# Cross-attention and a routed attention layer on one core: the order of operations around the routed attention and in the opening

## Chip, cores and metric

One core of a Trainium2 chip. The metric is the device time of one execution in microseconds (us); 64 batches are computed in it. Matrix products are done in float32 with operands split into two float32r parts ("hi" and "lo"), three products each.

## The reference

For each of 64 batches, x is 256 x 256 and the context 77 x 192. Layer 1 is cross-attention with 8 heads of 64; layer 2 is a causal attention whose queries, keys and values are mixed from 16 experts by routing weights.

```python
x = x + xattn(layernorm(x), ctx, Wq, Wk, Wv, Wo, bo)      # softmax(q k^T / 8) v, then Wo
h = layernorm(x)
logits = normalize(h) @ normalize(sim) - sigmoid(gates)   # 16 experts
rw = softmax of relu(logits) over the active experts (or the top 2 where none is)
q, k, v = [sum over e of rw[e] * (h @ proj[e]) for proj in (q_proj, k_proj, v_proj)]
attn = causal_softmax(q k^T / 8) v                        # one head of 64
x = x + sum over e of (attn * rw[e]) @ o_proj[e]
```

## The kernel before

The kernel is written engine by engine: each of the five engines has its own program, and every engine's order of work is written out by hand in a function `step(i)`, run for i = -2 to 65. Engines meet only in semaphores. Every engine works strictly through its list, so an operation that waits holds all that stands behind it on that engine. In step i the operations belong to batches i+2 (`nxt`), i+1 (`ahead`), i (`now`), i-1 (`before`) and i-2 (`earlier`), and where a batch does not exist they are left out.

**The cross-attention (names with a_)** is folded: for each group of three batches "jobs" turn the context into G (wq times keys) and U (values times Wo), which go through memory (`g_dram`, `u_dram`) and come back batch by batch as `gq` and `uo`. There are 25 jobs a group: ct, k 0 to 3, v 0 to 3, g 0 to 7, u 0 to 7. They are spread over the slots E0, E1, E2, E3, M1, M2, M3, L1, L2 of three consecutive steps by the table `JOBS`; a slot is run by `turn(...)`. Jobs g 3 to 7 fall in steps with i % 3 = 0, u 0 to 5 in those with i % 3 = 1, and u 6, u 7, k 0 to 2 and g 0 to 2 in those with i % 3 = 2. The A banks of PSUM (three) go round the slots in the order of `A_ORDER`, and `freed` waits for whoever held the bank before: S1 to S3, PT0 to PT2, XT, Y and the job slots share them. The bank of E3 is that of PT0 before it and of M2 behind it; PT1's passes to M1.

For one batch: ln1_a (bn_stats of `xt`, L1066) and ln1_b (L1081) normalise x, a_xT transposes it (XT), a_s 0 to 3 are the scores (S0 to S3), whose maximum DVE takes (L1163) and whose exponentials ScalarE takes (a_exp, L893); a_psum (L1170) gives the reciprocals of the sums, GpSimd multiplies (a_p, L1506), a_pT transposes (PT0 to PT2, L598, drained at L1175 and L1179), and a_y multiplies by `uo` (Y) and adds x.

**The routed attention.** ln2_a, ln2_b and b_norm normalise; b_xT transposes into banks of the B ring (L632); b_qkv 0 to 15 are the projections of two experts and one of the two token tiles each (L467 to L469), drained by DVE with the routing weights as factors (L1232 for 0 and 1, L1235 for the rest, two operations each). The B ring has three banks for 18 fills a batch, so b_qkv 3 waits until b_qkv 0 is drained, and b_xT 1 until b_qkv 14 of the batch before is. b_top (largest logits), b_index and GpSimd's b_route_1, b_route_2, b_w (L1476), then DVE's b_wsum (L1216, L1218) and GpSimd's b_rw (L1482) give the weights. c_qk transposes q and k (L658; four copies on ScalarE, two on DVE, L1246), c_s are the scores (L666), c_exp and c_p the softmax, c_pT its transpose (L674, drained at L1241), c_pv the product with v, c_mix 0 to 3 the products with the weights, and c_y the output projection, two steps later.

**The queues.** SyncE (SP) issues the loads and stores in order and waits in order: `load_x(n)` (L348), `load_ctx` (L358, L359), `store_g` (L364), `store_u` (L373), `load_g(n)` (L383, waits for all stores of G of the group), `load_u(n)` (L390 to L394, waits for all stores of U of the group), `store` (L399). ScalarE's queue issues the two small transfers that spread the routing weights over the partitions (`c_rT`, `c_rw`, L945 and L952).

**The opening.** Before step -2 the 25 jobs of group 0 are run in the order of `OPENING`, while the 16 weight pieces (`PIECES`: 0 to 5 the cross-attention's, 6 to 13 the experts' projections, 14 and 15 o_proj) are loaded into three staging areas and split into hi and lo (`split_weights`, L824 on ScalarE and L1051 on DVE) at the places that `SPLIT_AFTER` gives. A piece can be loaded only when the piece three before it is split.

Of the kernel before, what the change touches and what calls it, by code (L numbers as in the profile page):

```python
# [34 lines left out]
def xattn_moe_kernel(nc, x, ctx_in, Wq, Wk, Wv, Wo, bo, sim_matrix, gates, q_proj, k_proj, v_proj, o_proj, out, rw_dram):  # L35
# [63 lines left out]
    def on(n):  # L99
        return 0 <= n < B  # L100
# [14 lines left out]
    with es:  # L115
# [216 lines left out]
        def loads_before(piece):  # L332
# [4 lines left out]
                       ("u", 0): (9,), ("u", 2): (10,), ("u", 7): range(11, len(PIECES))}  # L337
# [5 lines left out]
        def _(sp):  # L343
# [33 lines left out]
            def load_g(n):  # L377
                gm, b = n // GB, n % GB
                for k in range(2):
                    sp.wait_ge(draft_out[k], stored(gm) + 16 * (H // 2))  # L380
                if n:
                    sp.wait_ge(s_fill, at(2 * NT, n - 1, 3))
                sp.dma_start(gq[:, :, :, :, :].rearrange("p a b c d -> p (a b c d)").bitcast(F32), g_dram[gm, b, :, :]).then_inc(g_in, 16)  # L383
# [35 lines left out]
            def step(i):  # L419
# [13 lines left out]
                if on(i + 2):  # L433
                    load_g(i + 2)
                turn("E1")
                if i % 3 == 2 and on(i + 1):
                    load_u(i + 1)
# [16 lines left out]
            for hc, pieces in enumerate(((12,), (13,), (), (14, 15))):  # L454
                store_u(0, 2 * hc)
                store_u(0, 2 * hc + 1)
                load_weights(pieces)
            for i in range(-2, B + 2):
                step(i)
# [4 lines left out]
        def _(pe):  # L464
# [270 lines left out]
            def step(i):  # L735
                nxt, ahead, now, before, earlier = [i + d for d in (2, 1, 0, -1, -2)]

                def do(n, fn, *k):
                    if on(n):
                        fn(n, *k)  # L740
# [55 lines left out]
                do(now, b_qkv, 1)  # L796
                do(before, c_s)
                do(now, b_qkv, 2)
                fill("Y", ahead, a_y, 0)
                do(before, c_pT)  # L800
                do(ahead, a_y, 1)
                do(before, c_pv)
                do(now, b_qkv, 3)
# [10 lines left out]
        def _(act):  # L814
# [164 lines left out]
            def step(i):  # L979
                nxt, ahead, now, before, earlier = [i + d for d in (2, 1, 0, -1, -2)]  # L980

                def do(n, fn, *k):
                    if on(n):
                        fn(n, *k)
# [16 lines left out]
                do(before, c_rT)  # L1001
                do(ahead, a_exp, 0)
                do(ahead, a_exp, 1)
                do(ahead, a_exp, 2)
                do(ahead, a_exp, 3)
                turn("E1")
# [4 lines left out]
                do(ahead, a_pT, 2)  # L1011
                turn("E3")
# [3 lines left out]
                do(nxt, a_xT)  # L1016
                turn("M2")
                do(before, c_qk)
                turn("M3")
                do(before, c_exp)  # L1020
# [15 lines left out]
        def _(dve):  # L1036
# [247 lines left out]
            def step(i):  # L1284
# [22 lines left out]
                do(before, b_qkv, 7)  # L1307
                do(now, ln2_a)
                do(ahead, a_s, 0)
                do(before, b_qkv, 8)  # L1310
                do(ahead, a_s, 1)
                do(now, ln2_b)
                do(before, b_qkv, 9)
                do(ahead, a_s, 2)
                do(now, b_norm, 0)
                do(before, b_qkv, 10)
                do(now, b_norm, 1)
                do(ahead, a_psum, 0)
                do(ahead, a_s, 3)
                do(now, b_norm, 2)  # L1320
                do(ahead, a_psum, 1)
                do(before, b_qkv, 11)
                turn("E1")
                do(earlier, c_y)
                turn("E2")
                do(nxt, ln1_a)
                do(before, b_qkv, 12)
# [3 lines left out]
                do(ahead, a_pT, 2)  # L1331
                do(nxt, ln1_b)
                do(before, b_qkv, 14)
                turn("E3")
                do(before, b_qkv, 15)
# [3 lines left out]
                do(nxt, a_xT)  # L1339
                turn("M2")  # L1340
                do(before, c_qk)
                do(now, b_top)
                do(before, c_s)
                do(now, b_index)
                do(before, c_p)
                turn("M3")
                do(before, c_pT)
# [3 lines left out]
                do(ahead, a_y)  # L1351
                do(before, c_mix, 0)
                do(now, b_qkv, 2)
                do(before, c_mix, 1)
                do(now, b_qkv, 3)
                do(before, c_mix, 2)
                do(now, b_qkv, 4)
# [212 lines left out]
```

## Time and profile before

| | |
|---|---|
| median of 3 runs | 2813.47 us (2812.5 to 2815.11) |
| the profiled execution | 2814.86 us, its span 2813.1 us |
| busy share of the span | PE 90%, DVE 78%, ACT 49%, POOL 39% |
| matmuls, transposes among them | 17308 |
| memory traffic | 157 GB/s over the span |
| chain that ended last | PE 59%, DVE 19%, ACT 12%, issue 7%, DMA 2%, POOL 1% |

PE is TensorE, DVE VectorE, ACT ScalarE, POOL GpSimd, SP SyncE. In the rows, `L1246` is a line of the kernel; "[0.93 <-DVE mixs_hi L1246]" says that the engine stood for 0.93 us and that the named instruction let it go ("issue" is a wait whose releaser the profile doesn't show, such as a load that landed). PEclk is the granted clock of TensorE as a share of 2.4 GHz; 0.50 is 1.2 GHz.

### The profile page before, as it was taken

How to read it: one execution, taken by the hardware profiler on the slowest of the kernel's cores; microseconds unless marked ns; L12 is line 12 of the kernel's file. 1: busy time of each engine (PE TensorE's matmuls, PEld its weight loads, DVE VectorE, ACT ScalarE, POOL GpSimd, SP SyncE). 2: the span in 40 equal slices, each digit the busy share in tenths (PEclk: the TensorE clock that was granted, in tenths of full speed). 3: DMA queues.
4: the chain of work that ended last, by engine and by line, in shares of the span. 5: the costliest groups of instructions: out<-in, count | busy, mean ns of one | idle time of the engine just before them, and what ended most of it. 6: DMA issues, size and time to landing. Idle time of an engine off the chain costs nothing.

```text
span 2813.1 us, 53794 instructions
## 1 busy us (share of the span) xinstructions
PE 2528.2 (90%) x17308; PEld 2427.3 (86%) x17308; DVE 2201.7 (78%) x6491; ACT 1378.8 (49%) x4598; POOL 1103.9 (39%) x1611
## 2 busy tenths in 40 slices
PE   4599999999999899999999999999989999999987
PEld 3589889889889889889889989988989988988986
DVE  5488888888888777878878878888778888888874
ACT  4454454555455454455455545545445455545531
POOL 0134344434434434434434434433434433443442
PEclk6699999999999999999999999999999999999998
DMA  7555555464555455455555555465555446455531
GB/s 188 186 158 169 172 165 160 139 189 142 172 170 161 149 165 164 137 184 154 168 163 169 155 157 177 133 186 155 169 159 163 156 146 189 139 173 167 161 91 41
DMA packets 299936, 445.75 MB, mean 158 GB/s; under 512 B 36857, under 2 KB 210873, under 8 KB 291465
## 3 DMA queue, kind: packets, MB, share of 16 engines
q1 hardware_dynamic: 230024, 374.15, 41.5%
q10 hardware_dynamic: 69632, 68.17, 10.9%
q8 instruction: 140, 2.29, 0.3%
q14 instruction: 140, 1.14, 0.1%
HBM read 257.91 MB, written 184.35 MB: 157 GB/s over the span
## 4 chain that ended last, share of the span: by engine, by line
PE 59%; DVE 19%; ACT 12%; issue 7%; DMA 2%; POOL 1%; SPq 0%; DVEq 0%; ACTq 0%; POOLq 0%
PE bank_b L467 9%; PE bank_b L469 8%; PE bank_b L468 8%; DVE acc L1235 5%; PE bank_a L467 4%; PE bank_c L467 4%; PE bank_c L469 4%; PE bank_c L468 4%; PE bank_a L468 4%; PE bank_a L469 4%; DVE both L1136 2%; DVE pT_lo L1179 2%; DVE probs L1081 2%; ACT both L852 1%; ACT both L851 1%
## 5 line engine op out<-in xcount | busy, mean ns | idle before, releaser
L467 PE MATMUL bank_b<-wqkv_hi,x2T_lo 128*128 128x384 f32 (+1 forms) x2048 | 724.7, 354 | 18.4 <-DVE acc L1232 18.1
L1235 DVE SCALAR_TENSOR_TENSOR acc<-bank_b,rw,acc 128x192 f32<-128x192 f32 x1792 | 659.7, 410 | 61.5 <-PE bank_b L469 54.9
L469 PE MATMUL bank_b<-wqkv_hi,x2T_hi 128*128 128x384 f32 (+1 forms) x2048 | 692.2, 338 | 0.0
L468 PE MATMUL bank_b<-wqkv_lo,x2T_hi 128*128 128x384 f32 (+1 forms) x2048 | 690.8, 337 | 0.0
L1511 POOL TENSOR_TENSOR mixs_lo<-mix,mixs_hi 128x512 fp32r<-128x512 f32 x256 | 404.1, 1609 | 227.0 <-ACT mixs_hi L961 227.0
L893 ACT ACTIVATE probs<-bank_a,s_max 128x77 f32<-128x77 f32 x1024 | 317.3, 330 | 281.8 <-DVE s_max L1163 279.2
L467 PEld LDWEIGHTS bank_b<-wqkv_hi,x2T_lo 128*128 128x128 f32 x2048 | 386.6, 189 | 29.5 <-DVE acc L1232 26.8
L468 PEld LDWEIGHTS bank_b<-wqkv_lo,x2T_hi 128*128 128x128 f32 x2048 | 387.9, 189 | 0.0
L469 PEld LDWEIGHTS bank_b<-wqkv_hi,x2T_hi 128*128 128x128 f32 x2048 | 384.6, 188 | 0.0
L1506 POOL TENSOR_TENSOR probs<-probs,p_sum 128x616 f32<-128x616 f32 x128 | 155.8, 1217 | 356.9 <-DVE p_sum L1170 356.9
L467 PE MATMUL bank_c<-wo_hi,mixs_lo 128*128 128x256 f32 x1024 | 288.6, 282 | 3.7 <-POOL mixs_lo L1511 3.7
L1436 POOL TENSOR_TENSOR pow_out<-pow_in,expo 128x2 f32<-128x2 f32 (+1 forms) x128 | 111.4, 871 | 452.2 <-DVE pow_in L1073 315.9
L469 PE MATMUL bank_c<-wo_hi,mixs_hi 128*128 128x256 f32 x1024 | 288.1, 281 | 0.0
L468 PE MATMUL bank_c<-wo_lo,mixs_hi 128*128 128x256 f32 x1024 | 287.7, 281 | 0.0
L961 ACT ACTIVATE mixs_hi<-mix 128x512 fp32r<-128x512 f32 x256 | 161.7, 632 | 231.4 <-DVE mix L1276 231.4
L1136 DVE TENSOR_TENSOR both<-bank_a,only 64x231 fp32r<-64x231 f32 x352 | 139.2, 395 | 141.3 <-ACT both L852 139.0
L1276 DVE TENSOR_TENSOR mix<-rw_all,late_tiles 128x512 f32<-128x512 f32 x256 | 231.8, 906 | 2.2 <-ACT late_tiles L957 2.1
L893 ACT ACTIVATION_READ_ACCUMULATOR probs<-bank_a,s_max 128x1 f32 x1024 | 215.4, 210 | 0.0
L467 PE MATMUL bank_a<-uo,pT_lo 128*128 128x256 f32 (+1 forms) x640 | 189.2, 296 | 18.1 <-issue 17.9
L467 PEld LDWEIGHTS bank_c<-wo_hi,mixs_lo 128*128 128x128 f32 x1024 | 193.4, 189 | 4.1 <-issue 3.8
L468 PEld LDWEIGHTS bank_c<-wo_lo,mixs_hi 128*128 128x128 f32 x1024 | 194.2, 190 | 0.0
L469 PEld LDWEIGHTS bank_c<-wo_hi,mixs_hi 128*128 128x128 f32 x1024 | 193.5, 189 | 0.0
(204 smaller groups left out, 6161.7 us busy)
## 6 DMA issues: line engine op xcount, KB each, us to landing
g_dram<-draft SPq DMA_DIRECT2D x176, 462.0 KB
gq<-g_dram SPq DMA_DIRECT2D x64, 1232.0 KB, 5.5
uo<-u_dram SPq DMA_DIRECT2D x64, 1024.0 KB
rw_all<-rw_dram ACTq DMA_DIRECT2D x128, 512.0 KB, 7.4
u_dram<-draft SPq DMA_DIRECT2D x176, 308.0 KB
xt<-in_x_dram SPq DMA_DIRECT2D x64, 256.0 KB, 3.9
out_dram<-mix SPq DMA_DIRECT2D x64, 256.0 KB, 6.2
u_dram<-draft SPq DMA_DIRECT2D x88, 156.0 KB
```

The costliest lines, as they stand in the source:

```text
L467: nc.tensor.matmul(dst, lhs[1], rhs[0], start=start, stop=False)
L468: nc.tensor.matmul(dst, lhs[0], rhs[1], start=False, stop=False)
L469: return nc.tensor.matmul(dst, lhs[0], rhs[0], start=False, stop=stop)
L893: last = nc.scalar.activation(probs[:, t, h * NC:(h + 1) * NC], bank_a(f"S{j}")[:, k * NC:(k + 1) * NC], ACT.Exp, bias=s_max[:, j, k:k + 1 ...
L961: nc.scalar.activation(mixs[0][:, 2 * j:2 * j + 2, :], mix[:, 2 * j:2 * j + 2, :], copy).then_inc(mix_hi, 1)
L1081: V.tensor_scalar(dst[:, t, :], src[:, t, :], mv[k][:, t, 0:1], pow_out[k][:, 0, t:t + 1], ALU.subtract, ALU.mult).then_inc(ln_done[k], 1)
L1136: last = V.tensor_tensor(both[rows, k, e, cols], src[rows, cols], only.bitcast(F32)[rows, k, e, cols], ALU.subtract)
L1235: V.scalar_tensor_tensor(acc[:, t, k, :], src, rw[:, t, e:e + 1], acc[:, t, k, :], ALU.mult, ALU.add).then_inc(b_evac, 1)
L1276: V.tensor_tensor(mix[:, 2 * j:2 * j + 2, :], rw_all[:, 2 * j:2 * j + 2, :], aT2[:, :].unsqueeze(1).to_broadcast([P, 2, T]), ALU.mult).the ...
L1436: G.tensor_tensor(dst, src, expo[:, 0:m], ALU.pow).then_inc(ln_pow[k], 1)
L1506: G.tensor_tensor(part, part, p_sum[:, half, 1, :, :].unsqueeze(3).to_broadcast([P, NT, HB, NC]), ALU.mult).then_inc(p_ready, 1)
L1511: G.tensor_tensor(mixs[1][:, 2 * j:2 * j + 2, :], mix[:, 2 * j:2 * j + 2, :], mixs[0].bitcast(F32)[:, 2 * j:2 * j + 2, :], ALU.subtract).t ...
```

## The change

No operation is added or removed and none changes its engine; orders change, in three places.

- On PE: b_qkv 2 goes ahead of c_s, c_pT behind both halves of Y, b_qkv 3 ahead of c_pv. On ScalarE: c_qk goes ahead of slot M2.
- On DVE: a_s 0 ahead of ln2_a; ln2_b two places later; ln1_a of the batch after next from behind slot E2 to the place between a_s 3 and the second a_psum; b_qkv 12 ahead of slot E2; ln1_b and b_qkv 15 ahead of slot E3 (ln1_b now behind b_qkv 14); c_qk ahead of M2; b_index ahead of c_s; c_pT from ahead of b_wsum to behind a_y; b_qkv 2, 3 and 4 each one place earlier among the c_mix.
- In the opening: pieces 11 to 15 are split inside step -1 instead of before step -2, on ScalarE and DVE; pieces 14 and 15 are loaded during step -1; load_g(0) is issued behind the stores of G and load_u(0) behind the stores of U.

```diff
--- before.py
+++ after.py
@@ -334,7 +334,7 @@
 
 
         SPLIT_AFTER = {("k", 1): (W_V,), ("k", 2): (W_O - 1, W_O), ("k", 3): (6,), ("v", 0): (7,), ("v", 1): (8,),
-                       ("u", 0): (9,), ("u", 2): (10,), ("u", 7): range(11, len(PIECES))}
+                       ("u", 0): (9,), ("u", 2): (10,)}
 
         block = es.enter_context(nc.Block())
 
@@ -430,10 +430,14 @@
                 turn("E0")
                 if on(i + 2) and i + 2 > 0:
                     load_x(i + 2)
-                if on(i + 2):
+                if i == -1:
+                    load_weights((14,))
+                if on(i + 2) and i + 2 > 0:
                     load_g(i + 2)
+                if i == -1:
+                    load_weights((15,))
                 turn("E1")
-                if i % 3 == 2 and on(i + 1):
+                if i % 3 == 2 and on(i + 1) and i + 1 > 0:
                     load_u(i + 1)
                 if on(i - 2):
                     store(i - 2)
@@ -451,10 +455,12 @@
                 store_g(0, 2 * hc)
                 store_g(0, 2 * hc + 1)
                 load_weights(pieces)
-            for hc, pieces in enumerate(((12,), (13,), (), (14, 15))):
+            load_g(0)
+            for hc, pieces in enumerate(((12,), (13,), (), ())):
                 store_u(0, 2 * hc)
                 store_u(0, 2 * hc + 1)
                 load_weights(pieces)
+            load_u(0)
             for i in range(-2, B + 2):
                 step(i)
             sp.wait_ge(y_out, 16 * B)
@@ -794,13 +800,13 @@
                 do(now, b_qkv, 0)
                 turn("M3")
                 do(now, b_qkv, 1)
+                do(now, b_qkv, 2)
                 do(before, c_s)
-                do(now, b_qkv, 2)
                 fill("Y", ahead, a_y, 0)
+                do(ahead, a_y, 1)
                 do(before, c_pT)
-                do(ahead, a_y, 1)
+                do(now, b_qkv, 3)
                 do(before, c_pv)
-                do(now, b_qkv, 3)
                 do(now, b_qkv, 4)
                 turn("L1")
                 do(now, b_qkv, 5)
@@ -999,24 +1005,34 @@
 
                 turn("E0")
                 do(before, c_rT)
+                if i == -1:
+                    split_weights(11)
                 do(ahead, a_exp, 0)
                 do(ahead, a_exp, 1)
                 do(ahead, a_exp, 2)
                 do(ahead, a_exp, 3)
+                if i == -1:
+                    split_weights(12)
                 turn("E1")
                 turn("E2")
                 do(ahead, a_pT, 0)
                 do(ahead, a_pT, 1)
                 do(before, c_rw)
                 do(ahead, a_pT, 2)
+                if i == -1:
+                    split_weights(13)
                 turn("E3")
                 do(now, b_xT, 0)
                 do(now, b_xT, 1)
                 turn("M1")
                 do(nxt, a_xT)
+                if i == -1:
+                    split_weights(14)
+                do(before, c_qk)
                 turn("M2")
-                do(before, c_qk)
                 turn("M3")
+                if i == -1:
+                    split_weights(15)
                 do(before, c_exp)
                 do(now, b_exp)
                 do(before, c_pT)
@@ -1305,56 +1321,66 @@
                 do(before, b_qkv, 6)
                 turn("E0")
                 do(before, b_qkv, 7)
+                if i == -1:
+                    split_weights(11)
+                do(ahead, a_s, 0)
                 do(now, ln2_a)
-                do(ahead, a_s, 0)
                 do(before, b_qkv, 8)
                 do(ahead, a_s, 1)
-                do(now, ln2_b)
                 do(before, b_qkv, 9)
                 do(ahead, a_s, 2)
-                do(now, b_norm, 0)
+                do(now, ln2_b)
                 do(before, b_qkv, 10)
-                do(now, b_norm, 1)
                 do(ahead, a_psum, 0)
                 do(ahead, a_s, 3)
+                do(now, b_norm, 0)
+                do(nxt, ln1_a)
+                do(now, b_norm, 1)
+                do(ahead, a_psum, 1)
                 do(now, b_norm, 2)
-                do(ahead, a_psum, 1)
                 do(before, b_qkv, 11)
+                if i == -1:
+                    split_weights(12)
                 turn("E1")
                 do(earlier, c_y)
+                do(before, b_qkv, 12)
                 turn("E2")
-                do(nxt, ln1_a)
-                do(before, b_qkv, 12)
                 do(ahead, a_pT, 0)
                 do(ahead, a_pT, 1)
                 do(before, b_qkv, 13)
                 do(ahead, a_pT, 2)
+                if i == -1:
+                    split_weights(13)
+                do(before, b_qkv, 14)
                 do(nxt, ln1_b)
-                do(before, b_qkv, 14)
+                do(before, b_qkv, 15)
                 turn("E3")
-                do(before, b_qkv, 15)
                 do(now, b_xT, 0)
                 do(now, b_xT, 1)
                 turn("M1")
                 do(nxt, a_xT)
+                if i == -1:
+                    split_weights(14)
+                do(before, c_qk)
                 turn("M2")
-                do(before, c_qk)
                 do(now, b_top)
+                do(now, b_index)
+                if i == -1:
+                    split_weights(15)
                 do(before, c_s)
-                do(now, b_index)
                 do(before, c_p)
                 turn("M3")
-                do(before, c_pT)
                 do(now, b_wsum)
                 do(now, b_qkv, 0)
                 do(now, b_qkv, 1)
                 do(ahead, a_y)
+                do(before, c_pT)
+                do(now, b_qkv, 2)
+                do(now, b_qkv, 3)
                 do(before, c_mix, 0)
-                do(now, b_qkv, 2)
                 do(before, c_mix, 1)
-                do(now, b_qkv, 3)
+                do(now, b_qkv, 4)
                 do(before, c_mix, 2)
-                do(now, b_qkv, 4)
                 do(before, c_mix, 3)
                 turn("L1")
                 do(now, b_qkv, 5)
```

## Rows read from the trace of the kernel before

**Rows 1.** The cores: span and mean granted clock of PE.

```profile
core 0: 2813.1 us, clock 0.978
```

**Rows 2.** PE's waits from 300 to 2650 us: total us, times, longest us.

```profile
PE bank_c L666 <- DVE mixs_hi L1246: 52.6, 56, 1.5
...
PE bank_b L632 <- DVE acc L1235: 47.8, 56, 0.9
...
PE bank_a L467 <- issue: 13.5, 16, 2.5
```

**Rows 3.** PE in order of time, kind 1: start, us, line, operation, [idle before <- releaser].

```profile
1042.31 0.38 PE L577 MATMUL bank_a<-wo,both 128*116 128x256 f32 x1 [0.83 <-DVE pT_lo L1179]
...
1047.21 0.41 PE L658 MATMUL bank_c<-ident,mix 128*128 128x128 f32 x2
```

**Rows 4.** DVE in order of time, the same step.

```profile
1039.60 0.75 DVE L1066 BATCH_NORM_STATS2 stats<-xt 128x6 f32<-128x256 f32 x2
...
1040.92 0.74 DVE L1235 SCALAR_TENSOR_TENSOR acc<-bank_b,rw,acc 128x192 f32<-128x192 f32 x2
```

**Rows 5.** PE, DVE and POOL in order of time, from c_s to b_qkv 3 of that step.

```profile
1051.20 0.30 PE L666 MATMUL bank_c<-mixs_hi 128*128 128x128 f32 x1 [0.93 <-DVE mixs_hi L1246]
...
1057.75 0.44 PE L467 MATMUL bank_b<-wqkv_hi,x2T_lo 128*128 128x384 f32 x1 [0.27 <-DVE acc L1232]
...
1055.68 0.56 DVE L1241 TENSOR_TENSOR mixs_lo<-bank_c,mixs_lo 128x384 fp32r<-128x384 f32 x1 [0.79 <-ACT mixs_lo L917]
...
1056.95 1.39 DVE L1232 TENSOR_SCALAR acc<-bank_b,rw 128x192 f32<-128x192 f32 x4 [0.42 <-POOL rw L1482]
...
1055.36 0.25 POOL L1476 TENSOR_TENSOR w<-w,act_on 128x32 f32<-128x32 f32 x1
```

**Rows 6.** SP, DVE, POOL and PE in a kind-2 step; then that x load's time to landing.

```profile
1073.94 0.40 SPq L348 DMA_DIRECT2D xt<-in_x_dram  x1
...
1078.58 0.66 SPq L373 DMA_DIRECT2D u_dram<-draft  x2
...
1088.08 0.38 SPq L392 DMA_DIRECT2D uo<-u_dram  x1
...
1074.29 0.48 DVE L1163 TENSOR_REDUCE s_max<-bank_a 128x4 f32<-128x308 f32 x1
...
1076.45 1.22 POOL L1506 TENSOR_TENSOR probs<-probs,p_sum 128x616 f32<-128x616 f32 x1 [0.80 <-DVE p_sum L1170]
...
1080.06 0.81 PE L598 MATMUL bank_a<-ident,probs 128*128 128x128 f32 x6
...
1095.13 0.35 PE L467 MATMUL bank_a<-uo,pT_lo 128*128 128x256 f32 x1 [0.98 <-issue]
...
1100.15 0.44 PE L467 MATMUL bank_b<-wqkv_hi,x2T_lo 128*128 128x384 f32 x1 [0.31 <-DVE acc L1232]
...
DMA to landing us min/median/max: 5.4/5.4/5.4
```

**Rows 7.** SP in a late kind-2 step; then the DMA queues from 1083 to 1085 us.

```profile
2459.50 0.66 SPq L373 DMA_DIRECT2D u_dram<-draft  x2
...
2465.91 0.38 SPq L392 DMA_DIRECT2D uo<-u_dram  x1
...
q10 hardware_dynamic: 440, 0.44, 96.5%
...
q1 hardware_dynamic: 51, 0.10, 13.1%
```

**Rows 8.** PE at Y of an earlier kind-2 step; then 969 to 974: busy us, PEclk, DMA share, GB/s.

```profile
968.51 0.36 PE L467 MATMUL bank_a<-uo,pT_lo 128*128 128x256 f32 x1 [2.52 <-issue]
...
969.00:974.00 5.00, 5.00 (x31) 5.00 (x31) 1.37 (x5) 0.49 (x1) 0.24 (x1) 0.66 0.04 12
```

**Rows 9.** PE and SP in the opening.

```profile
92.69 0.62 PE L467 MATMUL bank_a<-gq,xT_lo 128*128 128x308 f32 x1 [12.02 <-DVE cT_lo L1130]
...
89.62 0.39 SPq L348 DMA_DIRECT2D xt<-in_x_dram  x1
```

## The prediction

> **What bounds the kernel now.** I read the size of the run first: one core, 2813.1 us of span [rows 1]. The profiled execution took 2814.86 us around that span, 1.4 above the median of 2813.47; I work out a difference and take it from the median. TensorE (PE) is busy for nine tenths, so the second view is who PE waits for. Over 56 of the 64 steps [rows 2] three waits matter: c_s for VectorE's (DVE's) part of c_qk, 0.94 us a step; the transpose b_xT for the bank that b_qkv 14 leaves, 0.85 a step; and, about once in three steps, the attention product Y for the load of `uo`, 0.84. Steps come in three kinds by i % 3, which have different jobs of the context group in their slots; I call them kind 0, 1 and 2. A kind-1 step was followed instruction by instruction [rows 3 to 5], then a kind-2 step [rows 6].
>
> **Part 1, the stretch before b_xT (all kinds).** DVE drains PT0 late, because ln1_a of the batch after next (1.3 us, from 1039.60 to 1040.92), and b_qkv 12 after it, stand ahead of it [rows 4]. So PE stands 0.83 us in front of slot E3 and then 0.85 for the bank of b_qkv 14 [rows 2, 3]. The change puts ln1_a in front of the second reciprocal, where DVE otherwise waits for ScalarE's exponentials, and drains b_qkv 12 before slot E2 while ScalarE still works for it: that takes 1.9 us of DVE work out of the queue ahead of PT0, and both PE waits (1.7 us) go. What is late next: E3's result is now drained behind ln1_b and b_qkv 15, three times 0.6 to 0.75 us (the pair of acc operations in [rows 4] takes 0.74, and I take that for each), 2.0 us after b_qkv 14's, while PE needs E3's bank again at M2, two short jobs (about 1.0 us) after b_xT 1. A new wait of up to 0.9, less the 0.4 that c_qk gains because its sums on GpSimd (POOL) are ready first: net gain in kind 1, 1.2 us. In kind 0 the wait at E3 is nearly absent, but b_xT's wait and 0.3 in front of c_qk go: also 1.2.
>
> **Part 2, from c_qk to b_qkv 4.** PE does b_qkv 2 before c_s, which covers c_s's wait of 0.93, and ScalarE and DVE do c_qk before M2's job. But b_qkv 3 needs the bank of b_qkv 0, which DVE drains only with the routing weights: POOL's last product (1055.36 to 1055.61), DVE's sum, POOL's rw, then acc at 1056.95, and PE at 1057.75 [rows 5]. Before, that chain is held only by c_pT on DVE, from 1055.68 to 1056.16: moving c_pT behind a_y gives the chain 0.5 us and no more. And c_pv (three products, about 0.5 us) now follows b_qkv 3 and can no longer fill that wait. So PE loses its wait at c_s and gets one of about 1.6 in front of b_qkv 3: net 0 in kind 1, and 0.4 in kind 0, where b_index now comes ahead of c_s and gives POOL's chain its input sooner. c_pT on PE behind the whole of Y costs nothing while c_p takes less than Y's 3.5 us.
>
> **Part 3, kind 2.** ln1_a needs x of batch i+2, which SP loads in the same step, behind four context loads and two stores: issued at 1073.94, landed 5.4 us later, at 1079.3. The score maximum that stands ahead of ln1_a in the new order begins at 1074.29, so DVE arrives at 1074.7 and stands for 4.6 us [rows 6]. Queued behind it on DVE are the second reciprocal, b_qkv 11, slot E1 (which in this kind is u 7, the last of the group), c_y, b_qkv 12. Two things follow. POOL's product (1076.45, 1.22 us long) comes after 1080.6 + 0.3, so PT0 on PE moves from 1080.06 to 1082.4. And u 7 is drained and stored 3.8 us later than 1078.58. Only once all stores of the group have landed (1088.08) does SP load `uo`, which lets Y start at 1095.13 after 0.98 us of waiting [rows 6]. The store takes 9.5 us in this step, 6.4 in one of the last steps, which has no context loads [rows 7]. Bounds for Y: 3.8 + 6.4 - 9.5 = 0.7 later, and 3.8 later. I take 2.2, since the end of the store is tied to the `rw_all` loads on ScalarE's queue, which move with PT0 (2.3): while they run, they hold 96.5% of the engines and SP's queue 13.1% [rows 7].
>
> The Trainium skill ("DMA: Bandwidth & Descriptors", section on queues, rings and completion order) says that each DMA engine takes turns between the queues it has work for. By that rule the store would get a full share beside `rw_all` and land near the lower bound; the row at 13.1% is too small for even turns, but does not say whether the store had more to send.
>
> After Y, b_qkv 3 followed 5.0 us later in the old order (1100.15), held by the acc chain. With Y late that chain is long done: Y and c_pT take 3.9, so b_qkv 4 comes 0.6 sooner after Y than before. Loss in kind 2: 2.2 - 0.6 = 1.6 us, with bounds 0.1 and 3.2. Parts 1 and 2 gain nothing here, since Y's wait swallows what lies ahead of it. On top comes the clock. Where Y had waited 2.52 us, granted clock was 0.66 over the next 5 us, that is half rate (1.2 GHz) for a part of them, which costs 5 x 0.34 = 1.7 us [rows 8]. New waits here are 2.3 at PT0 and about 3.6 at Y. If the clock already falls after PT0, its cost vanishes in Y's wait; so bounds are 0 and 1.7, and I take 0.9.
>
> **Part 4, opening and end.** Five weight pieces are split inside step -1 rather than before step -2, and o_proj is loaded during it. DVE was behind them for the 12.02 us that S0 of batch 0 waited [rows 9]: that is the upper bound of the gain. But load_u(0) now stands on SP ahead of the context and x loads and waits for u 7's store, so x of batch 1 is issued about when it was before (89.62), and the new ln1_a waits for it ahead of the reciprocal. I take 4 us; the lower bound is a loss of 3, the five splits not fully hidden. At the end, the last two steps load no x and gain 2 together. Part 4: 6. The new issue order on SP costs nothing else; the exceptions at i == -1 move existing DMAs and add none.
>
> **Sum.** 20 kind-0 steps x 1.6 = 32 and 21 kind-1 steps x 1.2 = 25 gained; 20 kind-2 steps x (1.6 + 0.9) = 50 lost; 6 gained: net 13, so 2813.5 - 13 = 2801 us, 0.4% faster. Two large terms nearly cancel, so the sign hangs on kind 2.
>
> **Rivals.**
> A, the store of u 7 gets through (it no longer queues behind the 1.2 MB of `gq`; the page's rule speaks for it): kind 2 loses 0.1 and the wait stays short enough for the clock. 57 + 6 - 2 = 61 gained, 2752; with part of the late landing, 2765. Against it: `rw_all` begins sooner after that store than before. Chance 0.24.
> B, the other side: DVE's stop for x in kind 2 passes in full to Y, and PE's wait of 4 to 5 us drops the clock each time. 20 x (3.2 + 1.7) = 98 lost against 63: 35 slower, 2848. It decides from the point where kind 2 costs over 3.2 us a step (63 / 20). For it: clock did fall after each wait that I can show of over 2.4 us. Against: that store takes 6.4 us where nothing crowds it. Chance 0.27.
> C, parts 1 and 2 return as waits in full (M2 for E3's bank, b_qkv 3 for routing), so that kinds 0 and 1 gain only half: 28 + 6 - 34 = 0, with kind 2 somewhat milder at 1.7: no change, 2813. Chance 0.13.
> The forecast itself has 0.36, with a range of its own of 2788 to 2818.
>
> **How the numbers follow.** About 0.2% (5.6 us) is what a measurement of this kernel tells from no change. Faster by more than that: A whole (0.24), two thirds of the forecast (0.25), some of C (0.04): 0.53. Slower: B nearly whole (0.25), a sixth of the forecast (0.04) and C (0.03): 0.32. Same: 0.15. The range reaches from A to B, 2755 to 2845; about a tenth lies outside at each end.
>
> **What would show it.** Right: no PE wait for acc in front of b_xT and none for c_qk in front of c_s; instead one of some 1.6 us in front of b_qkv 3 in kinds 0 and 1, and up to 0.9 at M2. In kind 2, DVE idle for about 4.6 us in front of bn_stats of `xt`, released by the x load, PT0 released late by POOL, and Y's wait at 3 to 4 us with half-rate clock behind it in part of the steps. Period of three steps: 0.3 to 0.6 us shorter. Wrong: if x lands before DVE asks (then all kinds gain and the time is under 2755), if Y's start in kind 2 hardly moves (A), or if the clock also falls after the 1.6 us in front of b_qkv 3, where I count nothing: that would put the time above the range.

## The result and the profile after

The changed kernel takes 2932.47 us (median of 4 runs, 2928.24 to 2934.9) where the kernel before took 2812.98 beside it: ratio 1.0427, 95% interval 1.0406 to 1.0448. It is 4.3% slower; the forecast was 0.4% faster, and the time lies above the range.

The cores, then the busy times of the profiled execution (2933.07 us, its span 2931.2):

```profile
core 0: 2931.2 us, clock 0.945
...
PE 2606.9 (89%) x17308; PEld 2513.0 (86%) x17308; DVE 2321.8 (79%) x6491; ACT 1387.0 (47%) x4598; POOL 1085.2 (37%) x1611
```

Beside the 2813.1 us and the clock of 0.978 of before [rows 1], the span grew by 118.1 us. PE has the same 17308 instructions, and yet it is busy for 2606.9 us instead of 2528.2. **78.7 us of the 118.1 are the same products taking longer; only 39.4 are more standing still.** The first is the sign of the clock. PE's waits show both:

```profile
PE bank_a L473 <- issue: 72.1, 19, 4.6
PE bank_b L473 <- DVE acc L1248: 64.6, 37, 1.8
PE bank_a L604 <- POOL probs L1532: 19.3, 13, 2.5
PE bank_c L473 <- DVE mixs_lo L1257: 18.7, 52, 0.4
PE bank_a L571 <- DVE both L1152: 11.2, 19, 0.7
PE bank_a L546 <- DVE draft L1174: 10.1, 19, 0.5
PE bank_b L638 <- DVE acc L1251: 5.3, 17, 0.4
...
PE bank_c L680 <- DVE mix L1285: 1.2, 4, 0.5
```

(From 300 to 2760 us: total, times, longest. Lines are 6 higher than before on PE: L473 is the projection, Y and c_pv products, L604 PT0, L638 b_xT, L672 c_s, L680 c_pT; the bank_c line at L473 is c_pv.) Against [rows 2], the two largest waits of before are gone: c_s does not wait at all, and b_xT waits 5.3 us instead of 47.8. Their place is taken by Y, 3.8 us in each of 19 steps of kind 2, and by b_qkv 3, 1.75 us in each of 37 steps of kinds 0 and 1. Close behind it c_pv waits for DVE's drain of c_pT, 0.36 us in 52 steps. In order of time, a step of kind 0:

```profile
1051.53 0.52 PE L680 MATMUL bank_c<-ident,mix 128*128 128x128 f32 x3 [0.52 <-DVE mix L1285]
1053.54 0.69 PE L473 MATMUL bank_b<-wqkv_hi,x2T_lo 128*128 128x384 f32 x1 [1.49 <-DVE acc L1248]
1054.03 0.52 PE L474 MATMUL bank_b<-wqkv_lo,x2T_hi 128*128 128x384 f32 x1
1054.35 0.52 PE L475 MATMUL bank_b<-wqkv_hi,x2T_hi 128*128 128x384 f32 x1
```

The products of b_qkv 3 start 0.32 us apart and take 0.52, where they start 0.18 apart and take 0.34 a few microseconds later. The windows view says why (us, busy time of each engine, PEclk, DMA share, GB/s; first around b_qkv 3, then around Y of the kind-2 step before it, which starts at 1006.27 after 3.98 us):

```profile
1048.00:1053.00 5.00, 3.54 (x30) 3.12 (x28) 3.07 (x18) 1.60 (x6) 3.04 (x12) 1.00 0.48 112
1053.00:1058.00 5.00, 4.46 (x19) 4.46 (x20) 4.11 (x11) 0.38 (x1) 0.00 (x0) 0.66 0.66 237
1058.00:1063.00 5.00, 5.00 (x37) 4.96 (x36) 5.00 (x8) 2.83 (x5) 4.08 (x3) 1.00 0.01 3
...
1000.00:1005.00 5.00, 2.30 (x15) 2.09 (x13) 3.95 (x19) 1.86 (x7) 2.13 (x9) 1.00 1.02 305
1005.00:1010.00 5.00, 3.73 (x17) 3.76 (x18) 1.82 (x7) 0.00 (x0) 0.99 (x4) 0.56 0.50 164
1010.00:1015.00 5.00, 4.78 (x29) 4.49 (x28) 1.94 (x5) 0.49 (x1) 0.00 (x0) 0.76 0.10 26
```

A PEclk of 0.66 over 5 us is half rate (1.2 GHz) for a part of them, and takes 5 x 0.34 = 1.7 us from PE, the same loss as in [rows 8]; behind Y it is 2.2 + 1.2 = 3.4. I cut the span from 200 to 2690 us into windows of half a microsecond and summed what each lacked in PEclk: before, 2 such stretches and 3.4 us lost; after, **46 stretches and 97.2 us lost**. The loss is 1.7 or 3.4 each time. (It is above the 78.7 us of busy time; part of it falls where PE stands anyway.) Set beside PE's waits, 23 of the 46 lie at b_qkv 3, 19 at Y and 4 at PT0, where PE stands for 2.4 to 2.5 us in those steps of kind 2.

The third view is the mean time from one c_s to the next, by the kinds of the two steps (21 of each):

| kernel | 2 to 0 (holds kind 2's Y) | 0 to 1 | 1 to 2 |
|---|---|---|---|
| before | 42.01 | 41.61 | 41.03 |
| after | 43.86 | 42.35 | 44.12 |

The sum over three steps grew by 5.7 us, 21 times 5.7 = 119: the whole loss is in the steps, and none of it in the opening or at the end.

### The profile page after: what moved, and what is told of

Read it like the earlier page. It is cut to its first block, busy times and chain, and to the rows that moved or that the text cites. A ratio compares the mean times of both kernels' runs of the same rounds, so it can differ in the third digit from the quotient of the medians.

```text
span 2931.2 us, 53794 instructions
## 1 busy us (share of the span) xinstructions
PE 2606.9 (89%) x17308; PEld 2513.0 (86%) x17308; DVE 2321.8 (79%) x6491; ACT 1387.0 (47%) x4598; POOL 1085.2 (37%) x1611
## 4 chain that ended last, share of the span: by engine, by line
PE 58%; DVE 12%; issue 11%; ACT 7%; POOL 6%; ACTq 3%; DMA 2%; SPq 0%; DVEq 0%; POOLq 0%
PE bank_b L473 8%; PE bank_b L475 8%; PE bank_b L474 8%; PE bank_c L473 5%; PE bank_c L475 4%; PE bank_c L474 4%; PE bank_a L473 4%; PE bank_a L474 4%; PE bank_a L475 4%; ACTq L958 3%; DVE acc L1251 2%; POOL probs L1532 1%; PE bank_a L604 1%; DVE probs L1097 1%; ACT pT_hi L909 1%
## 5 line engine op out<-in xcount | busy, mean ns | idle before, releaser
L473 PE MATMUL bank_b<-wqkv_hi,x2T_lo 128*128 128x384 f32 (+1 forms) x2048 | 742.7, 363 | 74.9 <-DVE acc L1248 74.6
L475 PE MATMUL bank_b<-wqkv_hi,x2T_hi 128*128 128x384 f32 (+1 forms) x2048 | 705.6, 345 | 0.0
L474 PE MATMUL bank_b<-wqkv_lo,x2T_hi 128*128 128x384 f32 (+1 forms) x2048 | 702.9, 343 | 0.0
L1537 POOL TENSOR_TENSOR mixs_lo<-mix,mixs_hi 128x512 fp32r<-128x512 f32 x256 | 380.7, 1518 | 457.6 <-ACT mixs_hi L967 457.6
L473 PEld LDWEIGHTS bank_b<-wqkv_hi,x2T_lo 128*128 128x128 f32 x2048 | 397.0, 194 | 86.7 <-DVE acc L1248 84.8
L1292 DVE TENSOR_TENSOR mix<-rw_all,late_tiles 128x512 f32<-128x512 f32 x256 | 275.0, 1115 | 30.1 <-ACT late_tiles L963 30.1
L473 PE MATMUL bank_c<-wo_hi,mixs_lo 128*128 128x256 f32 x1024 | 288.7, 282 | 3.7 <-POOL mixs_lo L1537 3.7
L473 PE MATMUL bank_a<-uo,pT_lo 128*128 128x256 f32 (+1 forms) x640 | 200.9, 314 | 81.5 <-issue 80.9
L1517 POOL TENSOR_TENSOR mix<-acc 128x192 f32<-128x192 f32 x128 | 82.1, 641 | 427.2 <-DVE acc L1251 427.1
L473 PEld LDWEIGHTS bank_a<-uo,pT_lo 128*128 128x128 f32 (+1 forms) x640 | 140.8, 220 | 85.4 <-issue 84.6
L474 PE MATMUL bank_a<-uo,pT_hi 128*128 128x256 f32 (+1 forms) x640 | 197.8, 309 | 0.0
L475 PE MATMUL bank_a<-uo,pT_hi 128*128 128x256 f32 (+1 forms) x640 | 197.1, 308 | 0.0
```

Source lines behind the costliest of these rows:

```text
L473: nc.tensor.matmul(dst, lhs[1], rhs[0], start=start, stop=False)
L474: nc.tensor.matmul(dst, lhs[0], rhs[1], start=False, stop=False)
L475: return nc.tensor.matmul(dst, lhs[0], rhs[0], start=False, stop=stop)
L1292: V.tensor_tensor(mix[:, 2 * j:2 * j + 2, :], rw_all[:, 2 * j:2 * j + 2, :], aT2[:, :].unsqueeze(1).to_broadcast([P, 2, T]), ALU.mult).the ...
L1517: G.tensor_tensor(qkv[:, t, :], acc[:, t, 0, :], acc[:, t, 1, :], ALU.add).then_inc(qkv_ready, 1)
L1537: G.tensor_tensor(mixs[1][:, 2 * j:2 * j + 2, :], mix[:, 2 * j:2 * j + 2, :], mixs[0].bitcast(F32)[:, 2 * j:2 * j + 2, :], ALU.subtract).t ...
```

## The experiments

Twelve runs, in the order that the argument needs. Every time stands beside runs of the kernel before on the same chip, which had medians of 2812.6, 2813.8 and 2817.4 us in the three groups of runs; where runs of different groups are set against each other, I take ratios times 2813.5. Lists of PE's waits count from 300 to 2650 us unless another stretch is named.

**open_only: the opening alone (Part 4).** The kernel before with the changes of the opening, on SP, ScalarE and DVE, and with no change in the order of the steps.

```diff
-                if on(i + 2):
+                if on(i + 2) and i + 2 > 0:
                     load_g(i + 2)
...
+            load_g(0)
...
+                if i == -1:
+                    split_weights(11)
```

> Only the opening of the change (pieces 11 to 15 split in step -1, loads of o_proj, gq and uo reordered), all else as before. The clock theory and the x-load theory both put the loss in the steps: 2812, within 4 us of before, since the first c_s of the changed kernel came only 0.3 us sooner (172.70 against 172.98). A theory that the opening costs would want 10 us or more above before.

Measured: 2807.74 us (10 runs), ratio 0.9986 (0.9975 to 0.9997), clock 0.979. The opening gives about 4 us, as predicted, at the edge of what can be told from no change.

**mid_only: the middle alone (Part 2).** The kernel before with the new orders from M1 to L2; PE's part is shown, and ScalarE's and DVE's are those of the change.

```diff
                 do(now, b_qkv, 1)
+                do(now, b_qkv, 2)
                 do(before, c_s)
-                do(now, b_qkv, 2)
                 fill("Y", ahead, a_y, 0)
+                do(ahead, a_y, 1)
                 do(before, c_pT)
-                do(ahead, a_y, 1)
+                do(now, b_qkv, 3)
                 do(before, c_pv)
-                do(now, b_qkv, 3)
```

> Only the orders from M1 to L2 (b_qkv 2 ahead of c_s, c_pT behind Y, b_qkv 3 ahead of c_pv on PE; c_qk ahead of M2 on ScalarE and DVE; DVE's c_pT behind a_y). Clock theory: the waits of PE add up to about what they were, but one of about 1.6 us now stands in front of b_qkv 3, and the clock falls to half behind it in many steps: 30 to 80 us slower, 2845 to 2890, mean granted clock about 0.955. x-load theory (all the loss comes from ln1_a standing for x in the third kind of step): within 10 us of before, clock 0.978.

Measured: 2909.87 us, ratio 1.0342 (1.0322 to 1.0363), clock 0.955. PE's wait at b_qkv 3 from 300 to 2700 us:

```profile
PE bank_b L467 <- DVE acc L1232: 65.3, 41, 1.8
```

PE is busy for 2589.3 us, 61 more than before, and 31 half-rate stretches lose 63.1 us. So the part that I had put at a gain of 8 us costs 97: 61 of it in the clock, and 36 in PE standing more. That is over the 30 to 80 us expected. The 36 lie at c_pv, which waits 15.8 us where it waited for nothing, at Y, 31.8 us for 13.5, and in an exchange of c_s for b_qkv 3 that gained next to nothing (68.0 us for the two together before, 63.1 now, in fewer steps).

**early_only: DVE's early orders alone (Parts 1 and 3).** The kernel before with DVE's new order from E0 to M1, ln1_a early in all kinds.

> Only DVE's orders up to M1 (ln1_a early, b_qkv 12 ahead of E2, E3 behind b_qkv 15). Both theories: kinds 0 and 1 gain about 1.2 us a step (50 us); kind 2 loses about 2 us in front of Y and up to 3.4 by the clock. Clock theory: 2815 to 2860. x-load theory, which has to find 119 us here: 2900 or more.

Measured: 2868.63 us, ratio 1.0191 (1.0174 to 1.0208), clock 0.962; 25 half-rate stretches, 56.3 us lost. From 300 to 2700 us Y waits 58.3 us in 19 steps, and c_s 64.1 in 56. The time is 9 us above the expected 2815 to 2860, and 31 below the 2900 of the theory that all the loss lies here. The two parts alone, 97 + 56, are more than the 119 of the whole, so they are not independent; from here on they are taken one after the other.

**ln_late_k2: the changed kernel with ln1_a late in kind 2.** In that kind ln1_a goes back behind slot E2; all else is as changed.

```diff
-                do(nxt, ln1_a)
+                if i % 3 != 2:
+                    do(nxt, ln1_a)
...
                 turn("E2")
+                if i % 3 == 2:
+                    do(nxt, ln1_a)
                 do(ahead, a_pT, 0)
```

> The changed kernel with DVE's ln1_a early only in kinds 0 and 1, and in kind 2 (i % 3 = 2) where it was before. Clock theory: Y's wait in kind 2 falls back to about 1 us, but b_qkv 3's wait and its clock stay in kinds 0 and 1: 2810 to 2860. x-load theory: all that is lost comes back and the gain of the other steps shows: 2760 or less.

Measured: 2858.1 us, ratio 1.0172 (1.014 to 1.0205), clock 0.956. The one operation that stands for x in kind 2 costs 72 us by the ratios, 3.4 per kind-2 step, where Part 3 had 2.5 (1.6 and 0.9). The wait at b_qkv 3 is untouched (65.9 us in 38, from 300 to 2700 us), and 28 half-rate stretches are left, 20 at b_qkv 3 and 8 at Y.

**early_k01: the early orders in kinds 0 and 1, the middle as before.** The opening, DVE's early orders with ln1_a as in the run above, and the middle of the kernel before on all engines.

> Opening of the change, DVE's orders up to M1 with ln1_a early in kinds 0 and 1 only, and the orders from M1 to L2 as before the change. Clock theory: keeps the 1.2 us a step of part 1 and puts no wait over 1.5 us anywhere: 2750 to 2775, clock 0.975 or more. x-load theory the same. If part 1 by itself calls up dips of the clock (PE's two short waits now closer together in front of c_s): 2790 to 2830.

Measured: 2787.89 us (5 runs, 2775.07 to 2789.98), ratio 0.9886 (0.9868 to 0.9905), clock 0.974: faster than both kernels, though less than expected. What Part 1 gave at b_xT partly came back at c_s:

```profile
PE bank_c L672 <- DVE mixs_hi L1262: 64.3, 56, 3.2
PE bank_a L473 <- issue: 22.3, 19, 2.6
PE bank_b L473 <- DVE acc L1248: 14.7, 52, 0.5
```

b_xT waits only 5.7 us in 19 steps, but c_s waits 64.3 us where it waited 52.6 [rows 2]. These runs form a chain from before to after, each with one part more: opening -4; early orders in kinds 0 and 1 -28; the middle +80; ln1_a early in kind 2 +72. Together +120. (The last two are good to about 10 us by the intervals.) PE's busy time takes 43 of the 80 and 25 of the 72.

**filler: is it the clock?** The changed kernel with eight useless 384-column products on PE behind c_pT in every step, so that PE works while it would stand at b_qkv 3.

```diff
                 do(before, c_pT)
+                do(before, filler, 8)
                 do(now, b_qkv, 3)
```

> The changed kernel with 8 extra products of 384 columns on PE behind c_pT (about 0.17 us each, 1.4 us in all, written into the bank that c_pv overwrites), so that PE works through the wait in front of b_qkv 3. The work is useless and the waits of the other engines stay. Clock theory: the time lost by the clock behind b_qkv 3 goes, some 25 to 30 dips of 1.7 us: 2870 to 2890, although PE does 11 us x 8 more work (88 us busy). Theory that the waits themselves cost the time (the clock being only a mark of them): 2932 or more, up to 3000.

Measured: 2926.55 us, ratio 1.0404 (1.0388 to 1.042), clock 0.966. The expected 2870 to 2890 is missed, and the profile says by what:

```profile
PE bank_a L473 <- issue: 69.6, 18, 4.5
PE bank_a L604 <- POOL probs L1538: 37.3, 17, 2.8
...
PE bank_b L473 <- DVE acc L1254: 11.5, 33, 0.4
```

The wait at b_qkv 3 is nearly gone and half-rate stretches fell from 46 to 22 (44.4 us lost instead of 97.2), but 64 x 1.42 = 91 us of work were added, a third of it in kind 2, where b_qkv 3 doesn't wait, and PT0's wait doubled. Gain and price nearly cancel; as a test of the clock it is inconclusive by its time alone. The next two are cleaner.

**filler_k01: the same products in kinds 0 and 1 only.**

```diff
                 do(before, c_pT)
+                if i % 3 != 2:
+                    do(before, filler, 8)
```

> The changed kernel, with 8 useless products behind c_pT in the steps of kinds 0 and 1 only. The run with them in every step gave 2926.6 us: its waits at b_qkv 3 fell from 64.6 to 11.5 us and half-rate stretches from 46 to 22, but 64 times 1.45 us of products were added, 21 of these where nothing waited, and the 17 waits at the first transpose of the probabilities grew from 19.3 to 37.3 us. Theory: without the products of kind 2 the run gives back 21 x 1.45 = 30 us and perhaps the 18 us of the longer wait: 2878 to 2900 us, under the changed kernel's 2932 by 32 to 54 us although 43 x 1.45 = 62 us of useless work were added and only some 55 us of waiting taken out; the rest is the clock, 35 to 60 us. Rival (the clock is not worth anything by itself): within 10 us of the changed kernel, 2922 to 2942 us.

Measured: 2910.97 us, ratio 1.0335 (1.0317 to 1.0354), clock 0.963. The expected 2878 to 2900 is missed by 11 us, since PT0's wait stayed at 36.6 us instead of falling back: so it doesn't come from kind 2's products. That it comes from kinds 0 and 1 becoming faster is likely, but not shown. In sum: 43 x 1.45 = 62 us of products added, 52 of waiting at b_qkv 3 taken out, 17 more at PT0, and 51 fewer lost to the clock (46.1 in 23 stretches), which gives 24 less than the changed kernel; by the ratios it is 26. None of the 23 stretches left lies at b_qkv 3 (19 at Y, 4 at PT0). PE is busy for 2621.4 us, only 14.5 more than in the changed kernel, although 62 us of products were added: the other products took 48 us less. Adding useless work made the kernel faster.

**fill_y: the clock by itself.** The changed kernel with 20 such products in front of Y in kind 2, written to Y's own bank, which Y overwrites. Y waits for a load, so products that fit into its wait move nothing else.

```diff
+                if i % 3 == 2 and i > 0:
+                    fill("Y", ahead, filler, 20)
                 fill("Y", ahead, a_y, 0)
```

> The changed kernel, with 20 useless 384-column products put in front of Y in the steps of kind 2 (i % 3 == 2, from the third step on), into Y's own bank, which Y overwrites. In the changed kernel the 19 waits at Y between 300 and 2760 us take 72.1 us, 3.8 each, and what Y waits for is the load of uo, which TensorE does not set; 20 such products take about 3.5 us (8 took 1.5 in the run with the filler behind c_pT). So they fit into the wait and move nothing: what changes is only that TensorE works while it would stand. Theory (the stand itself costs the clock): the half-rate stretch behind Y, which costs 1.7 to 3.4 us in each step of kind 2, goes. 21 of them, 36 to 70 us: 2862 to 2897 us against the changed kernel's 2932; the mean granted clock rises from 0.945 to over 0.958. Rival (the clock falls for another reason, such as the load or the work as a whole): 2928 to 2940 us, clock under 0.95.

Measured: 2894.41 us, ratio 1.0279 (1.026 to 1.0299), clock 0.964: 42 us less than the changed kernel by the ratios, in the slower half of what the theory gave, with 21 x 3.66 = 77 us of work added. PE in order of time at one Y, then the windows around it, then the waits:

```profile
993.56 3.66 PE L686 MATMUL bank_a<-wqkv_hi,x2T_hi 128*128 128x384 f32 x20
997.64 0.36 PE L473 MATMUL bank_a<-uo,pT_lo 128*128 128x256 f32 x1 [0.42 <-issue]
...
999.00:1004.00 5.00, 4.77 (x38) 4.48 (x37) 2.85 (x8) 0.55 (x2) 0.00 (x0) 1.00 0.33 71
...
PE bank_b L473 <- DVE acc L1255: 64.2, 37, 1.8
...
PE bank_a L473 <- issue: 9.6, 17, 1.1
```

Nearly all of it is in the stretch that holds Y: from 43.86 us to 42.15 (2 to 0), while 0 to 1 (42.14) and 1 to 2 (44.15) differ by 0.2 us or less from the changed kernel. Y begins no sooner, counted from the load of x (24.6 us in the median of both). Half-rate stretches fell from 46 to 23, and 47.8 us are lost instead of 97.2. All 23 left lie at b_qkv 3. The two fillers split the 46 in two: those at Y and PT0 go when Y's wait is filled, those at b_qkv 3 when that one is.

**pv_first: c_pv ahead of b_qkv 3 again.** The changed kernel with this one order of PE undone, to see whether c_pv covers the wait as it did before.

```diff
-                do(now, b_qkv, 3)
                 do(before, c_pv)
+                do(now, b_qkv, 3)
```

> The changed kernel with c_pv ahead of b_qkv 3 on PE again (c_pT still behind Y, DVE's c_pT still behind a_y). Clock theory: c_pv has to wait for DVE's a_y and c_pT, so the wait moves in front of c_pv and stays at over 1 us; 0.5 us a step less: 2880 to 2915. If the place of c_pv alone is at fault: 2860 or less.

Measured: 3042.23 us, ratio 1.0812 (1.0796 to 1.0829), clock 0.935: 108 us slower than the changed kernel by the ratios, against my expectation of 2880 to 2915.

```profile
PE bank_c L473 <- DVE mixs_lo L1257: 144.0, 52, 3.6
```

c_pv needs DVE's drain of c_pT. The change put that drain behind a_y on DVE and c_pT behind Y on PE, so c_pv waits 2.8 us, and b_qkv 3 stands behind it; 62 half-rate stretches lose 131.4 us. I had moved one engine's order back and left the other two: an order on PE and the order of the drains on DVE are one thing.

**top_first: how long must the wait be?** As ln_late_k2, and DVE drains M2 only behind c_p, so that b_top starts POOL's routing chain sooner.

```diff
                 do(before, c_qk)
-                turn("M2")
                 do(now, b_top)
...
                 do(before, c_p)
+                turn("M2")
                 turn("M3")
```

> The changed kernel with ln1_a late in kind 2 and DVE's drain of slot M2 moved from ahead of b_top to behind c_p, so that the chain b_top, GpSimd's routing, b_wsum, rw, acc starts 0.6 to 1.3 us sooner. Theory that this chain sets b_qkv 3 and its wait sets the clock: the wait in front of b_qkv 3 falls from 1.7 to under 1 us and the dips in kinds 0 and 1 go: 2730 to 2780. If c_pT or the a_y drain ties b_qkv 3 instead: within 20 us of the 2858 of the run with ln1_a late alone.

Measured: 2809.48 us (11 runs), ratio 0.9993 (0.9983 to 1.0003), clock 0.972. It is 50 us faster than ln_late_k2 by the ratios, and 29 above the expected 2730 to 2780:

```profile
PE bank_b L473 <- DVE acc L1248: 49.5, 37, 1.5
PE bank_a L473 <- issue: 39.2, 19, 4.3
```

The wait at b_qkv 3 is 1.34 us each instead of 1.73, which is 15 us in all, and half-rate stretches fell from 28 to 14: from 20 to 7 at b_qkv 3, from 8 to 7 at Y. PE's busy time fell by 39.5 us. The chain of [rows 5] does set b_qkv 3, and with its wait 0.4 us shorter the clock fell there a third as often.

**qk_early and qk_top_early: the best of both.** The first is early_k01 with c_qk drained ahead of M2 on ScalarE and DVE; the second also has DVE's drain of M2 behind c_p.

```diff
+                do(before, c_qk)
                 turn("M2")
-                do(before, c_qk)
                 do(now, b_top)
```

> The run with the early orders in kinds 0 and 1 and the middle as before (2787.9 us), with one thing of the changed kernel's middle added: ScalarE and VectorE drain c_qk ahead of M2's bank. That run's largest wait of TensorE is c_s for the drain of c_qk, 64.3 us in 56 waits between 300 and 2650, 1.15 each. Theory (this wait can go without a price, since c_s stands behind b_qkv 1 and b_qkv 3 behind c_pv as before): c_s's wait falls under 10 us, M2's bank comes back later and costs under 10, b_qkv 3 waits no more than 0.5 us a time: 2730 to 2755 us, clock 0.97 to 0.98, faster than both kernels. Rival (the wait moves on to another place, since VectorE has as much to do): 2775 to 2795 us, with a wait of 0.8 us or more a step at b_qkv 3, Y or the key products.

> As the run before it, and on VectorE b_top, c_s and b_index also ahead of M2's drain, which moved behind c_p. In the changed kernel's middle this was worth 48 us, as it brought the routing weights and so b_qkv 3's bank back earlier. With the middle's products in the order of before, b_qkv 3 stands behind c_pv and hardly waits (14.7 us in 52 waits), so the theory expects nothing from it: within 8 us of the run with c_qk early, or up to 15 us slower where the late drain of M2 makes the key products wait. Rival (the routing chain still sets the pace): 15 us or more faster than the run with c_qk early.

Measured: 2766.63 us, ratio 0.9824 (0.9808 to 0.9839), and 2744.46 us, ratio 0.9744 (0.9728 to 0.9761), clocks 0.978 and 0.977. Some waits of PE, the first two lines of the first, the last two of the second:

```profile
PE bank_c L672 <- DVE mixs_hi L1262: 23.6, 38, 0.8
PE bank_c L680 <- DVE mix L1285: 17.4, 22, 1.2
...
PE bank_c L672 <- DVE mixs_hi L1262: 24.0, 39, 0.8
PE bank_b L473 <- DVE acc L1248: 15.8, 54, 0.5
```

c_s's wait fell from 64.3 us to 23.6, not under 10, so the first came out 12 us above its range. The second is 22 us faster than the first, where I had expected nothing. The rival was right in size but not in its reason: b_qkv 3's wait is 15.8 us in both. What went is c_pT's wait for c_p (L680, 17.4 us in 22), because c_s and c_p no longer stand behind the drain of M2; the time between c_s fell in 1 to 2 alone (41.58 to 40.62). Both have 4 half-rate stretches. The second is the fastest kernel here: 2.6% faster than before and 6.6% faster than the change.

## Why the prediction was wrong

**Part 4**: of its 6 us, the 4 of the opening were right (4 measured in open_only); the 2 of the end were not measured by themselves.

**Part 1** was right in its mechanism: b_xT's wait went (47.8 us to 5.3), and M2 waits for E3's bank for 0.24 to 0.59 us by kind of step where I had allowed 0.9. In size it was too large: 49 us on 41 steps, against 28 for the steps of kinds 0 and 1 in early_k01. There c_s took part of it back (64.3 us for 52.6), and 7 half-rate stretches instead of 2 lost 10 us more.

**Part 2 is the step that failed**, mostly by the clock and in part by its waits. The wait that it foresaw is there: c_s's is gone, and the new one in front of b_qkv 3 is 1.75 us for "about 1.6". The chain runs as the working had it (POOL's last product, DVE's sum, POOL's rw, acc). What failed is, first, that the clock was counted as nothing behind this wait. From 200 to 2690 us PE fell to 1.2 GHz there in 23 of 38 steps, in the changed kernel and in fill_y alike. Each fall costs 1.7 us or twice that, about as much as the stand itself. My last paragraph had named this as what would put the time above the range; it got no chance of its own. Second, the exchange "net 0 in kind 1, and 0.4 in kind 0" left out a wait: c_pv now stands for DVE's drain of c_pT, which had moved behind a_y. By kind, the mean waits at c_s, b_qkv 3 and c_pv together went from 1.75 us to 2.15 in kind 0 and from 1.2 to 2.2 in kind 1. The middle came to 80 us lost instead of 8 gained (97 by itself, 61 of them in PE's busy time).

A long wait does not bring the clock down by itself, however. The 0.94 us of c_s in [rows 2] is a mean: 1.47 in kind 0, 0.92 in kind 1, 0.43 in kind 2. So in the kernel before PE stood for 1.47 us in 20 steps from 200 to 2690 us, and the clock held behind every one of them. One of these stands, then the windows view around and behind it (PEclk is 1.00 in both):

```profile
1134.80 0.30 PE L666 MATMUL bank_c<-mixs_hi 128*128 128x128 f32 x1 [1.47 <-DVE mixs_hi L1246]
...
1133.00:1138.00 5.00, 3.53 (x27) 3.24 (x26) 3.91 (x19) 1.85 (x7) 2.12 (x8) 1.00 0.28 99
1138.00:1143.00 5.00, 4.74 (x37) 4.60 (x36) 3.34 (x10) 0.88 (x2) 0.99 (x4) 1.00 0.24 48
```

What differs at b_qkv 3 in the rows is that a second stand follows: c_pv's, 0.4 us long and 1.8 us later. Before, the next stand after c_s was b_qkv 3's 0.28 us, 6.5 us later. Whether the longer stand or the two close together bring the fall, no run separates.

The Trainium skill ("TensorE: Matmul & The Clock Gate", section "A second HAM failure mode: psum-queue depth-cycling") describes a kernel whose short idles between groups of products, from cycling PSUM banks, send the clock back and forth between its two levels and cost throughput between bursts. This case's trace agrees: b_qkv 3 waits for a bank of the B ring, 1.75 us, and 23 of the 46 stretches lie there.

**Part 3** had the right links and wrong sizes. DVE does stand for x (from 300 to 2760 us: total, times, longest; then SP and PE in a kind-2 step):

```profile
DVE stats L1082 <- DMA xt<-in_x_dram: 48.8, 18, 4.3
...
981.63 0.40 SPq L348 DMA_DIRECT2D xt<-in_x_dram  x1
...
990.04 0.66 SPq L373 DMA_DIRECT2D u_dram<-draft  x2
...
997.42 0.38 SPq L392 DMA_DIRECT2D uo<-u_dram  x1
...
1006.27 0.55 PE L473 MATMUL bank_a<-uo,pT_lo 128*128 128x256 f32 x1 [3.98 <-issue]
```

DVE stands 2.7 us at a time (18 waits), not 4.6: in the step shown x lands 5.6 us behind its issue, about as in [rows 6], but DVE comes to it later, for the last score maximum begins 2.6 us behind that issue where it began 0.35, and b_norm 0 follows it. PT0 waits 1.5 us in 13 steps, for 2.3. Against [rows 6], u 7 is stored 8.4 us behind the load of x instead of 4.6, 3.8 later as worked out; on the mean of the kind-2 steps it is 8.3 for 5.2. The store then takes 7.2 us instead of 8.6, inside the bounds of 6.4 and 9.5; but the load of `uo` takes until Y 9.0 instead of 7.65, and gives that gain back. Y comes 3.2 us later (24.6 for 21.45 behind the load of x), where I took 2.2. Rival A's half of this, that the store gets through, happened in part and was worth nothing. Y's wait is 3.8 us, for the 3.6 predicted, and the clock fell there every time, for 1.7 or 3.4 us and 2.2 on average, above the upper bound of 1.7. Kind 2 cost 72 us instead of 50: 47 for the 32 of waiting, 25 for the 18 of the clock. (Only that much of Y's clock belongs to Part 3; with ln1_a late Y already had 8 stretches.)

**The rivals.** B had the sign and its mechanism in kind 2, and its 2848 would have been about right without the middle: before, opening, early orders and ln1_a in kind 2 give 2813.5 - 4 - 28 + 72 = 2854. The 80 us of the middle were in no case.

**The miss in sum.** From 13 gained to 120 lost is 133 us. By the chain of runs, 88 of it are Part 2 (8 gained, 80 lost), 22 Part 3, 21 Part 1 and 2 Part 4. By PE's rows, the forecast had 31 us less of waiting and 18 lost to the clock; measured were 39.4 more of waiting and 78.7 of the clock. So both were off: the waits by 70 us, the clock by 61. (In the chances, "a sixth of the forecast" would be 0.06, not 0.04; nothing hangs on it.)

## What to carry to other kernels

When a change of orders makes one wait longer or moves waits closer together, its price can be more than the sum of the waits: read PEclk behind the longest waits, and price a stand by itself and by what the clock takes behind it. The sign to look for afterwards is PE's busy time: the same number of instructions with more busy time is a clock that fell. And an order on one engine can't be moved or undone without the order of the drains that feed it (pv_first); what paid here was to drain in the order in which PE asks next (c_qk ahead of M2, M2 behind c_p).

## What the runs showed of the hardware

Behind b_qkv 3, stands of 1.4 to 1.8 us were followed by the clock's fall to 1.2 GHz in half to two thirds of the steps: 23 of 38 in the changed kernel, 20 of 39 in ln_late_k2 (1.73 us each). In top_first 7 of 40 were, all of 1.43 us, and none of the 19 that were 1.31 us or shorter. The two fastest kernels have 4 half-rate stretches each, all at Y. The length of the stand doesn't decide it alone: stands of 1.79 us at b_qkv 3 were followed by a fall in some steps of one kernel and not in others, and the 20 stands of 1.47 us at c_s in the kernel before never were. What decides stays open.

That the stand is the cause, and not the load that runs beside it, is shown for Y by fill_y: the same load and the same start, with PE at work in place of the wait, and PEclk stayed at 1.00. For b_qkv 3 it is shown by filler_k01, where none of its 23 stretches is left. Each fall cost 1.7 us or 3.4 us and nothing between. Why the load of `uo` takes 1.4 us longer when the store ahead of it was shorter was not tried.
